# Separate calls for q, k and v of the second layer's attention, and a new order of calls, in a two-layer gated cross-attention kernel

## The reference

```python
x = x + tanh(g_xattn[0]) * L0_xattn(layernorm(x), ctx, ...)   # A
x = x + tanh(g_ffn[0])   * L0_ffn(layernorm(x), ...)          # B
x = x + tanh(g_xattn[1]) * L1_xattn(layernorm(x), ctx, ctx, ...)  # C
x = x + tanh(g_ffn[1])   * L1_ffn(layernorm(x), ...)          # D

# A: two attentions with one head, x to context and context to x, and a gate that mixes them
gate = sigmoid(concat([char2sub, sub2char]) @ Wg.T + bg)
A = gate * char2sub + (1 - gate) * sub2char
# B: top 1 of 8 experts, each a 256 x 256 matrix with a bias, times the winner's probability
# C: 16 heads of 16
q = proj(query, Wq, bq); k = proj(key, Wk, bk); v = proj(value, Wv, bv)
q = q * cos + rotate_half(q) * sin
k = k * cos + rotate_half(k) * sin
attn_w = softmax(einsum('bhqd,bhkd->bhqk', q, k) * scale)
C = einsum('bhqk,bhkd->bhqd', attn_w, v) @ Wo + bo
# D: top 2 of 8 experts, gelu between two matrices, every expert computed and weighted
```

## Time and profile before

| | |
|---|---|
| median of 3 runs | 519.73 us (517.99 to 520.77) |
| the profiled execution | 514.42 us |
| its span in the trace | 513.1 us |
| mean granted TensorE clock over the span | 0.959 of full |
| TensorE busy | 470.4 us, 92% |
| VectorE, ScalarE, GpSimd busy | 69%, 66%, 55% |
| chain that ended last | TensorE 77%, VectorE 6%, ScalarE 5% |

### The profile page before, as it was taken

One profiled execution on the slowest core, in us unless ns is written; L12 is line 12 of the kernel. 1 busy time (PEld: TensorE's weight loads), 2 busy tenths in 40 slices (PEclk: granted clock), 3 DMA queues, 4 the chain that ended last, 5 costly groups with the idle time before them and its releaser, 6 DMA issues.

```text
span 513.1 us, 11114 instructions
## 1 busy us (share of the span) xinstructions
PE 470.4 (92%) x3918; PEld 408.2 (80%) x3918; DVE 351.9 (69%) x873; ACT 338.1 (66%) x691; POOL 282.1 (55%) x362
## 2 busy tenths in 40 slices
PE   3999999989999968299987799999999999999996
PEld 3899999979988867186754488698797978888896
DVE  6757776697636764848555778776774785966485
ACT  3587888866666524344255588888778758688843
POOL 2435573675524386665278767846757454432264
PEclk9999999998999986689999699999999999999999
DMA  6999100112447432778847143130500503000001
GB/s 204 300 365 367 66 22 3 31 53 82 135 150 215 140 104 66 201 237 248 268 139 248 59 168 85 60 112 20 164 27 1 190 22 126 25 2 24 1 22 41
DMA packets 41783, 61.51 MB, mean 120 GB/s; under 512 B 5134, under 2 KB 22912, under 8 KB 41728
## 3 DMA queue, kind: packets, MB, share of 16 engines
q1 hardware_dynamic: 35872, 52.67, 32.4%
q0 software_dynamic: 1536, 4.20, 2.7%
q10 hardware_dynamic: 4320, 3.93, 2.2%
HBM read 26.21 MB, written 17.43 MB: 85 GB/s over the span
## 4 chain that ended last, share of the span: by engine, by line
PE 77%; DVE 6%; ACT 5%; issue 5%; POOL 4%; DMA 2%; SPq 0%; POOLq 0%; DVEq 0%; ACTq 0%
PE psum L382 16%; PE psum L384 14%; PE psum L383 14%; PE psum L615 6%; PE psum L549 6%; PE psum L389 4%; PE psum L586 4%; PE psum L603 4%; ACT PT L1355 2%; PE psum L550 2%; PE psum L539 2%; PE psum L624 1%; PE psum L560 1%; PE psum L423 1%; POOL yg L2790 1%
## 5 line engine op out<-in xcount | busy, mean ns | idle before, releaser
L2218 DVE TENSOR_REDUCE mpad<-psum 128x4 f32<-128x1024 f32 x64 | 76.6, 1219 | 22.1 <-PE psum L586 21.0
L1355 ACT ACTIVATE PT<-psum 128x1024 f32<-128x1024 f32 x64 | 64.1, 1024 | 21.3 <-PE psum L603 18.7
L2749 POOL TENSOR_TENSOR wA<-stage,wA 128x512 fp32r<-128x512 f32 x32 | 41.3, 1291 | 53.0 <-ACT wA L1402 50.6
L2287 DVE SCALAR_TENSOR_TENSOR xall<-psum,gat,xall 128x256 f32<-128x256 f32 x112 | 46.6, 476 | 7.1 <-PE psum L384 3.9
L382 PE MATMUL psum<-wB,wA 128*128 128x256 f32 x128 | 38.7, 302 | 0.0
L382 PE MATMUL psum<-x4h,wB 128*128 128x256 f32 x128 | 37.6, 294 | 0.0
L615 PE MATMUL psum<-PT,vv 128*32 128x256 f32 x512 | 36.0, 401 | 1.3 <-ACT PT L1355 1.3
L2736 POOL TENSOR_TENSOR parts<-qp,parts 128x512 fp32r<-128x512 f32 x16 | 20.8, 1299 | 29.6 <-ACT parts L1348 29.6
L383 PE MATMUL psum<-wB,wA 128*128 128x256 f32 x128 | 35.9, 281 | 0.0
L384 PE MATMUL psum<-wB,wA 128*128 128x256 f32 x128 | 35.8, 280 | 0.0
L384 PE MATMUL psum<-x4h,wB 128*128 128x256 f32 x128 | 35.8, 280 | 0.0
(11 more groups left out here) (284 smaller groups left out, 1751.5 us busy)
## 6 DMA issues: line engine op xcount, KB each, us to landing
st<-parts SPq DMA_DIRECT2D x48, 256.0 KB, 2.6
wt<-exp_d SPq DMA_DIRECT2D x30, 256.0 KB, 2.9
slots_d<-ys SPq DMA_DIRECT2D x3, 2304.0 KB
stage<-mats_d SPq DMA_DIRECT2D x21, 256.0 KB, 3.5
cx<-ctx_d SPq DMA_DIRECT2D x16, 256.0 KB, 3.3
qr<-qp SPq DMA_DIRECT2D x32, 128.0 KB
xs<-slots_d SPq DMA_DIRECT2D x30, 128.0 KB, 3.1
y_d<-ys ACTq DMA_DIRECT2D x30, 128.0 KB, 2.7
```

The source lines that it names most:

```text
L1355: e.activation(PT[:, i:i + 2, :, :].rearrange("p a k n -> p (a k n)"), ps2("ST", b, j).rearrange("p a n -> p (a n)"), ACT.Exp, scale=0.25) ...
L2218: e.tensor_reduce(mpad[:, :, 0:16].rearrange("p t (o a) -> p t o a", a=8)[:, :, :, j], ps2("max", b, j).rearrange("p o (t n) -> p t o n", ...
L2287: e.scalar_tensor_tensor(out=xall[:, b, t, :], in0=ps("dn", b, x)[:, t * 256:(t + 1) * 256], scalar=gat[:, b % 2, t, x:x + 1], in1=xall[:, ...
L2749: e.tensor_tensor(hlo[:, i, :], stage[:, n % 4, :], hh[:, i, :].bitcast(F32), ALU.subtract).then_inc(h_lo, 1)
```

## The change

The two calls `c_qk` and `c_v` become three, `c_k`, `c_v` and `c_q`. `c_k` and `c_v` wait for the context's low part, `c_q` for x's. The semaphore `t_cproj` that counted all three projections becomes `t_kv` and `t_q`. The bias of k now comes before that of q. And the lists of calls of all five engines are written anew, with other banks; no call is added or dropped but for the split.

```diff
-        t_cproj, a_qp, a_vv = sem("t_cproj"), sem("a_qp"), sem("a_vv")
+        t_kv, t_q, a_qp, a_vv = sem("t_kv"), sem("t_q"), sem("a_qp"), sem("a_vv")
...
             if what == "qk":
-                return a_qp, 2 * b + at[1] + 1
+                return a_qp, 2 * b + 2 - at[1]
...
-            def c_qk(b, *at):
-                for i, (n, act) in enumerate([("wq", X), ("wk", C)]):
-                    o = take(at[i], "qk", b, i)
-                    w.wait_ge(v_xl["C"], b + 1)
-                    w.wait_ge(c_lo, AT["C", b] + 1)
-                    w.wait_ge(*w_of(n))
-                    times_w(o, n, act).then_inc(t_cproj, 1)
+            def c_k(b, at):
+                o = take(at, "qk", b, 1)
+                w.wait_ge(c_lo, AT["C", b] + 1)
+                w.wait_ge(*w_of("wk"))
+                times_w(o, "wk", C).then_inc(t_kv, 1)
 
             def c_v(b, at):
                 o = take(at, "cv", b)
+                w.wait_ge(c_lo, AT["C", b] + 1)
                 w.wait_ge(*w_of("wv"))
-                by_w(o, "wv", C).then_inc(t_cproj, 1)
+                by_w(o, "wv", C).then_inc(t_kv, 1)
+
+            def c_q(b, at):
+                o = take(at, "qk", b, 0)
+                w.wait_ge(v_xl["C"], b + 1)
+                w.wait_ge(*w_of("wq"))
+                times_w(o, "wq", X).then_inc(t_q, 1)
...
                 elif was == "C":
-                    w.wait_ge(t_cproj, 3 * at + 1)
+                    w.wait_ge(t_q, at + 1)
...
                 elif was == "C":
-                    w.wait_ge(t_cproj, 3 * (at + 1))
+                    w.wait_ge(t_kv, 2 * (at + 1))
...
-            def qk_bias(b):
-                for i, n in enumerate(["wq", "wk"]):
-                    w.wait_ge(t_cproj, 3 * b + i + 1)
-                    w.wait_ge(r_lo, 2 * b)
-                    w.wait_ge(d_qr, 64 * b)
-                    for k in range(2):
-                        last = e.activation(qp[:, i, k, :], ps("qk", b, i)[:, k * 256:(k + 1) * 256], ACT.Identity,
-                                            bias=vec[:, VEC[n] + k:VEC[n] + k + 1])
-                    last.then_inc(a_qp, 1)
+            def with_bias(i, n, b):
+                w.wait_ge(r_lo, 2 * b)
+                w.wait_ge(d_qr, 64 * b)
+                for k in range(2):
+                    last = e.activation(qp[:, i, k, :], ps("qk", b, i)[:, k * 256:(k + 1) * 256], ACT.Identity,
+                                        bias=vec[:, VEC[n] + k:VEC[n] + k + 1])
+                last.then_inc(a_qp, 1)
+
+            def k_bias(b):
+                w.wait_ge(t_kv, 2 * b + 1)
+                with_bias(1, "wk", b)
+
+            def q_bias(b):
+                w.wait_ge(t_q, b + 1)
+                with_bias(0, "wq", b)
 
             def v_copy(b):
-                w.wait_ge(t_cproj, 3 * b + 3)
+                w.wait_ge(t_kv, 2 * b + 2)
                 w.wait_ge(t_O, 4 * (b - 2))
                 w.wait_ge(v_vv0, 2 if b == 0 else 4)
                 e.activation(vv[b % 3][:, :, :, 0:16], ps("cv", b).rearrange("p (t h d) -> p t h d", t=2, d=16), ACT.Copy).then_inc(a_vv, 1)
```

TensorE's list at the hand-over from layer 0 to layer 1:

```diff
             moe_w(14)
+            ln_T("B", 6, 1)
             rank(4, 0)
-            gate(7, 1)
-            ln_T("B", 6, 0)
-            route_B(6, 2)
-            mix(7, 0)
-            rank(5, 1)
-            rank(6, 3)
-            ln_T("B", 7, 2)
+            gate(7, 2)
+            rank(5, 0)
+            route_B(6, 1)
+            c_k(0, 3)
+            rank(6, 2)
+            mix(7, 1)
+            ln_T("B", 7, 3)
             ln_T("C", 0, 0)
             route_B(7, 1)
-            c_qk(0, 2, 0)
-            rank(7, 3)
-            c_v(0, 0)
-            ln_T("C", 1, 1)
-            c_qk(1, 0, 1)
-            moe_T(15, 0)
-            moe_T(16, 2)
-            c_v(1, 3)
+            c_v(0, 2)
+            c_q(0, 0)
+            rank(7, 1)
+            ln_T("C", 1, 3)
+            c_k(1, 0)
+            c_q(1, 1)
+            moe_T(15, 2)
+            c_v(1, 0)
+            moe_T(16, 3)
+            moe_T(17, 4)
             moe_w(15)
-            moe_T(17, 1)
             moe_w(16)
             moe_w(17)
             moe_T(18, 0)
```

ScalarE's list, at the start and at the first batches of C. `bo_hi` stood further on:

```diff
+            bo_hi()
             w_hi("g1")
...
             x_hi("C", 1)
             part_hi(0, 0)
             part_hi(1, 0)
-            qk_bias(1)
+            k_bias(1)
+            ln_apply("C", 2)
+            q_bias(1)
             xs_T(15)
-            ln_apply("C", 2)
+            ctx_hi("C", 2)
             xs_T(16)
```

VectorE's list, at the hand-over and in the first exponentials:

```diff
             c_stats(1)
             x_lo("C", 0)
             b_top(7)
-            add_moe(2)
             slots(7)
             alloc(1)
             turned(0)
             turned(1)
+            add_moe(2)
             x_lo("C", 1)
+            c_stats(2)
+            st1_init()
             add_moe(3)
-            c_stats(2)
             c_stats(3)
             y_out(15)
             y_out(16)
...
             add_moe(4)
+            c_stats(4)
             head_max(7, 1)
-            c_stats(4)
             add_moe(5)
+            max_parts(1)
             normed(0)
-            max_parts(1)
             o_lo(0)
```

GpSimd's list:

```diff
             out_lo(0, 7)
+            ln_rstd("B", 6)
             out_lo(1, 7)
-            ln_rstd("B", 6)
             sum_diff(7)
             scatter(4)
             rex_in(5)
             gather(0)
+            gather(1)
             gate_B(5)
-            gather(1)
             ln_rstd("B", 7)
+            rex_in(6)
             ln_rstd("C", 0)
+            scatter(5)
             gather(2)
-            scatter(5)
-            rex_in(6)
             scatter(6)
             scatter(7)
             ln_rstd("C", 1)
```

SyncE's list:

```diff
+            load_x(5)
             load("wq")
-            load_x(5)
+            load("wk")
             load("wv")
-            load_ctx("A", 2)
-            load_x(6)
             load_ctx("A", 3)
             zero_slots(1)
-            load("wk")
+            load_ctx("A", 4)
+            load("r")
...
-            load_ctx("C", 0)
             load_tile(0)
             load_tile(1)
             load_tile(2)
+            load("wo")
+            load_ctx("C", 1)
+            load_ctx("C", 0)
             load_tile(3)
-            load("wo")
             load_tile(4)
             load_tile(5)
             load_tile(6)
...
+            load_ctx("C", 2)
             swap_halves(0)
+            load_tile(15)
             load_tile(16)
+            load_tile(18)
             load_tile(17)
-            load_tile(15)
-            load_tile(18)
             stack(0)
```

More of the change, by code:

```diff
@@ L849, in tensor_program @@
             moe_T(21, 0)
+            c_q(2, 2)
             moe_w(21)
             moe_T(22, 1)
-            c_qk(2, 2, 3)
+            c_k(2, 3)
             moe_w(22)
-            moe_T(23, 0)
-            ln_T("C", 3, 2)
+            c_max(6, 0, 4)
+            ln_T("C", 3, 0)
+            c_v(2, 2)
+            moe_T(23, 3)
+            moe_T(24, 0)
             moe_w(23)
-            c_max(6, 0, 4)
-            moe_T(24, 1)
-            c_v(2, 3)
             moe_w(24)
-            moe_T(25, 0)
+            moe_T(25, 1)
             c_max(7, 0, 4)
@@ L864, in tensor_program @@
             moe_w(25)
-            moe_T(26, 3)
+            moe_T(26, 0)
             c_maxT(0, 2)
@@ L869, in tensor_program @@
             c_max(2, 1, 6)
-            c_qk(3, 1, 0)
-            moe_T(27, 4)
-            c_max(3, 1, 6)
-            moe_T(28, 2)
+            c_k(3, 3)
+            c_q(3, 2)
+            moe_T(27, 1)
+            c_max(3, 1, 4)
+            moe_T(28, 0)
             moe_w(27)
             c_max(4, 1, 6)
-            moe_T(29, 5)
+            moe_T(29, 4)
             moe_w(28)
@@ L909, in tensor_program @@
             c_PV(1, 1)
-            c_max(4, 2, 4)
-            c_exp(5, 1, 6)
+            c_exp(5, 1, 4)
+            c_max(4, 2, 6)
             ln_T("C", 4, 1)
-            c_max(5, 2, 4)
-            c_exp(6, 1, 6)
-            c_PV(2, 1, 3)
+            c_exp(6, 1, 4)
+            c_max(5, 2, 6)
+            c_PV(2, 1, 2)
+            c_k(4, 3)
             c_max(6, 2, 4)
             c_exp(7, 1, 6)
-            c_qk(4, 1, 0)
-            ln_T("D", 0, 2)
+            ln_T("D", 0, 0)
+            c_q(4, 1)
             c_PV(3, 1)
             c_max(7, 2, 4)
-            route_D(0, 2)
-            d_up(0, 0, 0)
+            route_D(0, 0)
+            d_up(0, 0, 3)
             d_up(1, 0, 1)
-            c_v(4, 3)
-            d_up(2, 0, 2)
-            c_maxT(2, 0)
+            c_v(4, 2)
+            d_up(2, 0, 0)
+            c_maxT(2, 3)
             c_max(0, 3, 4)
@@ L959, in tensor_program @@
             c_PV(3, 2)
-            c_max(7, 3, 4)
+            c_max(7, 3, 6)
             d_down(6, 0, 3)
-            d_up(0, 1, 0)
+            d_up(0, 1, 1)
             d_up(1, 1, 2)
-            c_maxT(3, 0)
+            c_maxT(3, 1)
             route_D(1, 3)
-            c_qk(5, 2, 0)
+            c_k(5, 2)
+            c_q(5, 1)
             c_max(0, 4, 4)
```

(22 more changed lines are left out.)

938 lines of the change are left out of this document (469 added, 469 removed).

## The result

The changed kernel is slower: 522.75 us against 518.30 us, medians of 20 runs each; the ratio is 1.0076, with a 95% interval of 1.0057 to 1.0096. The forecast was 518.4 with a range of 512.8 to 522.6, and a gain of 1.35 us. The slower side had 0.21 there.

What follows compares the result with a forecast made beforehand. TensorE's waits and low clock at the layer hand-over (184 to 222 us) and layer 1's first exponentials (276 to 300) were taken as the bound; −0.6 and −0.75 summed to −1.35 us, giving 518.4, range 512.8 to 522.6.

Steps and rivals of the forecast that it cites:

- (f): All other moves, among them first loads, initialisations, context loads, biases and changed PSUM banks: costed at nothing.
- (a): Hand-over between layers, ahead of ln_T("C", 0): reordered calls cost +0.7 us, the later statistics of B, 7 mostly hidden.
- (b): Hand-over, ln_T("C", 0) to rank(7): v takes k's place ahead of q, −0.2 us, leaving +0.5.
- (c): Hand-over, c_k(1) ahead of c_q(1): k runs in an idle gap, −1.3 us at moe_T(15), with 0.9 for add_moe(2).
- (d): Clock in the hand-over: half of the gain comes back, −0.6 us counted for (a) to (d).
- (e): Layer 1's first exponentials, max_parts(1) before normed(0) on VectorE: TensorE's 0.76 us wait goes, −0.75 us.
- Rival 1: First exponentials of layer 1: the clock's fall from 287 to 297 us goes too, 514.9 us; chance 0.27.
- Rival 3: Hand-over, VectorE before xl: add_moe(2) meets GpSimd's low part and takes 1.9 us, 522.4 us; chance 0.20.

Runs made afterwards that it cites:

- e6: The change with the order and banks of before up to moe_w(14), about the first 180 us, on all five engines: ratio to before 1.0036.
- e2: e1 plus the new order and banks of the first 180 us, the order of before behind it: ratio to before 1.0163.
- e1: Before with c_qk split into c_k and c_q side by side, old order of calls, k in its old bank: ratio to before 1.0103.
- e13: The change with proj_lo("vc", 5), which makes vcl, and b_top(3) ahead of row_max(0, 5) and row_max(1, 5) on VectorE: ratio to before 0.9991.
- e8: Before with one swap on VectorE, b_top(3) ahead of row_max(1, 5): ratio to before 0.9921.
- e3: e1 plus the new order of the hand-over alone, about 180 to 230 us: ratio to before 1.0092.
- e12: The change with before's first 180 us, mix(7) and rank(6) ahead of c_k(0), c_q(0) and rank(7) ahead of c_v(0): ratio to before 0.9973.
- e5: Before with c_qk split into c_k and c_q, old order of calls, banks of k and q swapped: ratio to before 0.9972.
- e10: Before with one swap on VectorE, max_parts(1) ahead of normed(0): ratio to before 0.9999.
- e15: The change with add_moe(2) moved back ahead of slots(7) on VectorE: ratio to before 1.0060.

## Why the prediction was wrong

**(f), costed at nothing, failed first.** The forecast took the first 180 us as free of waits and held that "each call still finds one emptied long ago in TensorE's full stretches", of the banks. proj("t0", 6) does not: it waits 3.27 us for bank 0, until `vcl` has emptied it, and the clock falls for longer (0.72 instead of 0.86). `vcl` is that late because it stands behind a scaling that GpSimd holds for 4.04 us. The forecast named such a hold in the hand-over but did not look for it elsewhere, where before's trace had one of 3.15 us with a wait of 2.44 us behind it. Without the new first 180 us the change is 0.40%, 2.1 us, faster (e6; e2 against e1 says 0.6%), and with three calls moved on VectorE, which takes `vcl` and b_top(3) out of the hold, it is at 0.9991 (e13). That the hold costs is shown; that the bank is needed for it is read from the two traces and the code. But e13 must be set against e8, the same repair of before (0.9921): the 0.7% between them lie behind 180 us. What stood among the marks of a wrong prediction, "if TensorE waits anywhere between 20 and 180 us", is what happened.

**Behind 180 us the loss is 0.36%, 1.9 us, against a forecast gain of 1.35** (e6; by e13 and e8 it is 0.7%). Its cause is not shown. The largest delay there that a trace can point at is one that before's trace does not have:

**(a) was right, and something else came on top.** Its terms were 0.7 us at ln_T("C", 0), and "VectorE's statistics of B, 7 are that much later", about 2 us, "hidden, with only a few tenths left". mix(7) is 2.0 us later behind tile 14 (8.54 against 6.50), as it said. In e3 that is hidden as it said: ln_T("B", 7) is 0.7 late. In the change VectorE stands another 2.1 us between mix(7) and its product. The statistics are then 3.3 us late (13.0 behind tile 14 against 9.7), GpSimd, which came to them when forecast (11.2 against 11.0), stands for 1.93, and ln_T("B", 7) is 2.5 us late. Why VectorE stands there is open.

**(b) held against before**: rank(7) comes 2.4 us late in the change, all of it from the gap on VectorE and (a); in e3, 0.6 late against a forecast of 0.5. That another order of v, q and rank(7) would do better, e12 makes likely and its interval does not settle.

**(c) had the right mechanism.** It put c_k(1) near 213, which is 33 behind tile 14 (34.84 measured), and c_q(1) 1.4 us late, of which 0.9 for add_moe(2). add_moe(2) took 0.87. c_q(1) came 3.25 us late (39.42 against 36.17), which is about 2.4 from (a) and 0.9 from add_moe(2). In e3, without the gap, c_q(1) is 1.5 late and moe_T(15) 1.1 early, against 1.4 and 1.2 in the forecast. Taken by itself, with neither delay, the split should have given the 12 matmuls' 2.6 us: e5's trace has 2.5 at moe_T(15), and its time 0.28%, 1.45 us.

**(d) came out as a loss**: with (a) late the low clock lasted to 228 us, 44 us behind tile 14, before to 222, 42 us behind it. moe_T(15) was 0.7 us late instead of 1.2 early. In e3 it was 1.1 early, but no run shows that this reaches the end of the kernel: e3's time is like e1's.

**(e), −0.75, is not settled by the time** (e10, 0.9999 with an interval of some 1.2 us to either side). In its trace the c_exp is 0.45 us earlier, of the 0.76. Its sentence "what is late next is ScalarE's exp" named what takes the wait's place.

**The rivals.** Rival 1 was to be decided by the clock's fall near 287 us. In the changed kernel it is gone from there, but it has only moved, to 280 and 305 us, and the time did not come; in e10, with (e) alone, it stays. Rival 3 was on the right side with the wrong place: add_moe(2) met no stall (0.87 us, e15), and TensorE was late from VectorE's gap behind mix(7) and, ahead of it all, from 112 us. Its chance held "every other new stall in the reordered first 180 us" as an afterthought; that was the main case.

## What to carry to other kernels

Before a list of calls is reordered, look through the whole trace for short instructions on VectorE with a duration out of all proportion (two numbers in 3 us) beside a run of GpSimd instructions: what stands behind such an instruction is late by the rest of the run, and a swap of two calls there was worth 0.8%. For each call whose PSUM bank changes, look up who held the bank and which instruction empties it, and when that one runs: in e1 the bank brought back the very wait that the split took away, and cost 1%, and in the change it made proj("t0", 6) wait 3.27 us for a tensor that it does not read. And before a difference between two traces is put down to the order of calls, look for a trace with the same calls: the 2.2 us at the start and the 2.1 us behind mix(7) are in the change's trace and missing in others with its calls.
